# A recurrent layer whose input products are read from PSUM on VectorE, and a sparse layer whose front starts inside its last two steps

## What is computed

```python
def _lru_forward(x, ...):                       # all 4096 rows, D = 256
    u = einsum('btd,edh->ebth', x, W_in) + b_in
    in_r, in_i, o = u[0], u[1], u[2]
    nu, theta, gamma = exp(params_log)
    lam = exp(complex(-nu, theta))
    uc = complex(gamma * in_r, gamma * in_i)
    h = associative_scan(h_t = lam * h_{t-1} + uc_t)
    out = h.real @ W_mid[0] - h.imag @ W_mid[1] + (b_mid) + o
    y = gelu(out @ w1_w + w1_b) @ w2_w + w2_b + out
    return (y - mean) * rsqrt(var + eps) * ln_g + ln_b

def _gated_bottleneck(x2d, ...):                # the sparse layer's front
    xc = einsum('ngf,gf->ng', x2d.reshape(n, g, 4), conv_w) + conv_b
    xn = batchnorm over all rows of xc
    return gelu(xn) @ lin_w.T + lin_b           # scores for a top 32
```

## Time and profile before

| | us |
|---|---|
| median of 3 runs | 1512.84 (1508.34 to 1513.26) |
| the profiled execution's own time | 1514.08 |
| its span, first to last instruction | 1512.4 |
| granted TensorE clock, mean | 0.948 |

### The profile page before, as it was taken

How to read it: one execution, slowest core, us unless ns; L and a number is a source line. 1 busy time by engine, 2 the same in 40 slices (tenths; PEclk the granted TensorE clock), 3 DMA queues, 4 the chain that set the end, 5 groups by cost and what they waited for, 6 DMA issues and landing times.

```text
span 1512.4 us, 30887 instructions
## 1 busy us (share of the span) xinstructions
PE 1273.1 (84%) x10332; PEld 780.5 (52%) x10332; DVE 1175.4 (78%) x2857; ACT 1119.0 (74%) x2453; POOL 1027.2 (68%) x1137
## 2 busy tenths in 40 slices
PE   4879998877777779999999999999999999767665
PEld 2435544534445435556666566665666567334343
DVE  7989888369989978777777667776777653699997
ACT  3424333487887759998988888888888895888886
POOL 3476886328877768776777667776676772188887
PEclk9989999979899989999999999999999999799997
DMA  6100000000000000000000000000000000000000
GB/s 186 39 1 0 1 0 0 1 0 1 1 1 1 1 1 2 2 2 2 2 2 2 2 2 2 2 1 2 2 2 2 2 2 1 0 15 29 15 29 29
DMA packets 26280, 14.70 MB, mean 10 GB/s; under 512 B 14406, under 2 KB 25868, under 8 KB 26124
## 3 DMA queue, kind: packets, MB, share of 16 engines
q1 hardware_dynamic: 26124, 12.74, 3.2%
HBM read 8.47 MB, written 4.19 MB: 8 GB/s over the span
## 4 chain that ended last, share of the span: by engine, by line
PE 41%; DVE 17%; issue 15%; POOL 13%; ACT 12%; DVEq 0%; DMA 0%; SPq 0%; POOLq 0%; ACTq 0%
POOL arena L692 5%; PE banks L1715 5%; PE banks L1727 4%; PE banks L1729 4%; PE banks L1654 3%; PE banks L1677 3%; DVE arena L1294 3%; ACT arena L1006 3%; DVE arena L1196 3%; PE banks L1744 3%; DVE arena L1289 2%; PE banks L1601 2%; PE banks L1746 2%; PE banks L1745 2%; ACT arena L1014 2%
## 5 line engine op out<-in xcount | busy, mean ns | idle before, releaser
L692 POOL TENSOR_TENSOR arena<-arena 128x512 f16<-128x512 f32 x384 | 439.5, 1161 | 191.1 <-ACT arena L1014 188.7
L1006 ACT ACTIVATE arena<-banks 128x512 f32<-128x512 f32 x512 | 303.9, 599 | 85.5 <-PE banks L1729 80.7
L1380 DVE TENSOR_REDUCE arena<-banks 128x1 f32<-128x1024 f32 x256 | 309.7, 1217 | 11.0 <-PE banks L1715 7.8
L1014 ACT ACTIVATE arena<-arena 128x512 f16<-128x512 f32 x512 | 316.0, 631 | 0.1
L1744 PE MATMUL banks<-arena 128*128 128x65 f16 x2048 | 214.7, 195 | 11.9 <-POOL arena L692 11.9
L1744 PEld LDWEIGHTS banks<-arena 128*128 128x128 f16 x2048 | 190.6, 97 | 49.4 <-issue 22.3
L1745 PE MATMUL banks<-arena 128*128 128x64 f16 x2048 | 214.9, 192 | 0.0
L1746 PE MATMUL banks<-arena 128*128 128x65 f16 x2048 | 214.0, 193 | 0.0
L1397 DVE TENSOR_TENSOR arena<-arena 128x512 f16<-128x512 f32 x128 | 101.8, 796 | 141.3 <-ACT arena L1014 141.3
L1294 DVE MATCH_REPLACE8 arena<-arena 128x256 f32<-128x256 f32 x512 | 204.7, 405 | 0.7 <-issue 0.6
L1745 PEld LDWEIGHTS banks<-arena 128*128 128x128 f16 x2048 | 190.1, 99 | 27.4 <-issue 0.3
(11 more groups left out here) (201 smaller groups left out, 2757.6 us busy)
## 6 DMA issues: line engine op xcount, KB each, us to landing
x<-in_L_attn_a_x SPq DMA_DIRECT2D x8, 512.0 KB, 4.0
out<-x SPq DMA_DIRECT2D x8, 512.0 KB, 3.0
arena<-arena SPq DMA_DIRECT2D x64, 1.0 KB, 1.9
arena<-in_L_attn_a_W_in SPq DMA_DIRECT2D x1, 768.0 KB, 5.8
arena<-in_L_attn_a_W_mid SPq DMA_DIRECT2D x1, 512.0 KB, 6.7
arena<-in_L_attn_a_w_w SPq DMA_DIRECT2D x2, 256.0 KB, 6.9
arena<-in_L_attn_b_Wq SPq DMA_DIRECT2D x1, 512.0 KB
arena<-in_L_attn_b_Wo SPq DMA_DIRECT2D x1, 512.0 KB
```

Source lines behind the costliest of these rows:

```text
L692: nc.gpsimd.tensor_tensor(pr_lo[c][:, kt, :], pr[:, kt, :], pr_hi[c][:, kt, :], ALU.subtract).then_inc(a_lP, 1)
L1006: nc.scalar.activation(pr[:, kt, :], ps[6 + kt % 2][:, :], ACT.Exp, scale=SM_SCALE).then_inc(a_P, 1)
L1014: nc.scalar.activation(pr_hi[c][:, kt, :], pr[:, kt, :], ACT.Copy).then_inc(a_hi, 1)
L1380: nc.vector.tensor_reduce(mx[c][:, j:j + 1], psum[:, 2 * pair:2 * pair + 2, :].rearrange("p a b -> p (a b)"), X, ALU.max).then_inc(a_mx, 1)
```

## The change

- **PSUM read on VectorE.** ScalarE's `lru_u` is gone. VectorE's `turned_in` reads the input products out of PSUM with scalar_tensor_tensor, (ps + bias) * table, eight instructions of 128 x 512 in place of GpSimd's `products_in` and VectorE's two products. `sums` adds them up.
- **Gamma in the weights.** gamma is loaded as a row over all partitions (`gam`, one more DMA), exponentiated by ScalarE ahead of Sin, and multiplied into W_in's first two parts by GpSimd (`s_scaled`). decT is made on GpSimd, the sign of w_mid on ScalarE.
- **y.** `gain` and ScalarE's normalisation out of PSUM become `centred` on VectorE, (y - mean) * ln_g out of PSUM, and a scaling by rstd on ScalarE. `rstd2` has two instructions, not four. Banks 6 and 7 are free after `centred`.
- **Orders.** ScalarE copies outT before it normalises. VectorE's order in a step: `sums(n+1)`, half the scans, `stats2(n-1)`, `centred(n-1)`, the other scans, `turned_in(n+2)` first half, `turned_back(n+1)`, `turned_in(n+2)` second half, then statistics. The conv matrix is made in step 3, the bias rows in steps 4 and 5. The setup transposes of TensorE use two banks, not four.
- **The sparse front.** Chunks 0 to 3 are normalised, turned and partly multiplied inside steps 6 and 7 (`front_turn`, `feature_chunk`, `front_rows`, `features`); the others follow.

The diff, cut (SyncE's list, carvings, semaphores and repeated wait numbers left out):

```diff
@@ gpsimd
-            def products_in(n, c):
-                ur, ui = u[c]
-                pool.wait_ge(l_u, n * 4 + 4)
-                ...
-                nc.gpsimd.tensor_tensor(pa, ur, cosT, ALU.mult).then_inc(l_pool, 1)
-                nc.gpsimd.tensor_tensor(pb, ui, cosT, ALU.mult).then_inc(l_pool, 1)
+            def turned_back(n, part):
+                pool.wait_ge(l_dve, n * L_STEPS + 4)
+                nc.gpsimd.tensor_tensor((pa, pb)[part], g[0], (cosT, sinT)[part], ALU.mult).then_inc(l_pool, 1)
             ...
+            pool.wait_ge(s_win, 16)
+            pool.wait_ge(s_gam, 17)
+            scaled = win[:, 0:2, :, :].rearrange("p e k h -> p (e k) h")
+            nc.gpsimd.tensor_tensor(scaled, scaled, gam.unsqueeze(1).to_broadcast([P, 2 * KB2, D]),
+                                    ALU.mult).then_inc(s_scaled, 1)
             ...
             def lru_step(n, c, behind, ahead1, ahead2, ahead4):
                 if ahead1:
-                    products_in(n + 1, 1 - c)
+                    turned_back(n + 1, 0)
                 if behind:
                     rstd2(n - 1)
                 if ahead1:
-                    products_out(n + 1)
+                    turned_back(n + 1, 1)
@@ scalar
             def lru_yhat(n):
-                act.wait_ge(l_r2, n * 4 + 4)
-                ...
+                act.wait_ge(l_r2, n * 2 + 2)
                 for j in range(TPC):
-                    nc.scalar.activation(yhat[:, j, :], ps[6 + j // 2][:, D * (j % 2):D * (j % 2) + D],
-                                         ACT.Identity, bias=ynmr[:, j:j + 1],
+                    act.wait_ge(l_yc, n * TPC + j + 1)
+                    nc.scalar.activation(yhat[:, j, :], yhat[:, j, :], ACT.Copy,
                                          scale=yrs[:, j:j + 1]).then_inc(l_y, 1)
             ...
             def lru_step(n, c, behind, ahead1, ahead2, ahead4):
                 if ahead2:
                     lru_z(n + 2, c)
-                if behind:
-                    lru_yhat(n - 1)
+                if n == NCH - 2:
+                    front_rows(0)
+                if n == NCH - 1:
+                    zT_chunk(LN_FFN1 + 1, 1, 2)
+                    front_rows(2)
                 for m in range(KB2):
                     ...
-                if ahead2:
-                    lru_u(n + 2, c, (0, 1))
+                if n >= NCH - 2:
+                    zT_chunk(LN_FFN1 + 2 * (n - NCH + 2), 0, 0)
+                if behind:
+                    lru_yhat(n - 1)
                 for m in range(KB2):
                     ...
-                if ahead2:
-                    lru_u(n + 2, c, (2, 3))
+                if n >= NCH - 2:
+                    front_rows(2 * (n - NCH + 2) + 1)
             ...
-            first_rows()
+            zT_chunk(LN_FFN1 + 3, 1, 2)
+            front_rows(4)
+            zT_chunk(LN_FFN1 + 4, 0, 0)
+            front_rows(5)
             lru_yhat(NCH - 1)
+            for m in range(5, NCH):
+                zT_chunk(LN_FFN1 + m, m % 2, 2 * (m % 2))
+                if m + 1 < NCH:
+                    front_rows(m + 1)
@@ vector
+            def turned_in(n, qs):
+                wait_from(dve, l_dve, (n - 1) * L_STEPS + 2)
+                for q in qs:
+                    e, m = q // 2, q % 2
+                    dve.wait_ge(l_ups, n * 4 + q + 1)
+                    for part, table in enumerate((cosT, sinT)):
+                        nc.vector.scalar_tensor_tensor(out=turned[e][part][:, m, :], in0=ps[u_bank(n, q)][:, :],
+                                                       scalar=gbias[:, q:q + 1], in1=table[:, m, :],
+                                                       op0=ALU.add, op1=ALU.mult).then_inc(l_u, 1)
+
+            def centred(n):
+                wait_from(dve, l_x, n)
+                dve.wait_ge(l_st2, n * 8 + 8)
+                ...
+                for j in range(TPC):
+                    nc.vector.scalar_tensor_tensor(out=yhat[:, j, :],
+                                                   in0=ps[6 + j // 2][:, D * (j % 2):D * (j % 2) + D],
+                                                   scalar=ymv[:, j, 0:1], in1=lng,
+                                                   op0=ALU.subtract, op1=ALU.mult).then_inc(l_yc, 1)
             ...
             def lru_step(n, c, behind, ahead1, ahead2, ahead4):
                 if ahead1:
-                    turned_in(n + 1, 1 - c)
+                    sums(n + 1)
+                    scan(n + 1, 1 - c, 0)
                 if behind:
                     stats2(n - 1)
+                    centred(n - 1)
                 if ahead1:
-                    scans(n + 1, 1 - c)
-                if behind:
-                    gain(n - 1)
+                    scan(n + 1, 1 - c, 1)
+                if ahead2:
+                    turned_in(n + 2, (0, 1))
+                if ahead1:
+                    turned_back(n + 1, 1 - c)
+                if ahead2:
+                    turned_in(n + 2, (2, 3))
                 ...
+                if n == NCH - 1:
+                    features(0, 1)
                 if behind:
                     dve.wait_ge(l_x, n)
                     next_stats((n - 1) * TPC, (n - 1) * TPC, n - 1, TPC)
+                if n == 3:
+                    conv_matrix()
+                if n == 4:
+                    bias_row(0, 0)
+                    bias_row(32, 0)
+                if n == 5:
+                    bias_row(64, 1)
+                if n >= NCH - 2:
+                    features(0, 2 * (n - NCH + 2))
@@ tensor
             def lru_u(n, c, qs):
                 ...
-                    if not (isinstance(n, int) and n == 0 and q < 2):
-                        pe.wait_ge(l_u, n * 4 + q - 1)
+                    if n:
+                        pe.wait_ge(l_u, n * 8 + (2 * q - 2 if n > 2 or n == 2 and q > 1 else 2 * q - 6))
             ...
             def lru_step(n, c, behind, ahead1, ahead2, ahead4):
                 ...
+                if n >= NCH - 2:
+                    front_turn(n - NCH + 2)
                 ...
+                if n >= NCH - 2:
+                    feature_chunk(0, n - NCH + 2)
+                if n == NCH - 1:
+                    front_turn(2)
                 pe.wait_ge(l_o, n * 4 + 4)
-                pe.wait_ge(l_y, n * 4 + CREDIT["l_y"])
+                wait_from(pe, l_yc, n * TPC)
                 ...
+                if n == NCH - 1:
+                    feature_chunk(0, 2)
+                    front_turn(3)
                 pe.wait_ge(l_y1, n * 2 + 2)
```

More of the change, by code:

```diff
@@ L137, in hybrid_block_kernel @@
         lnb = carve([D])
+        gam = carve([D])
         sinT = carve([KB2, CH])
         decT = carve([KB2, CH])
-        u = [[carve([KB2, CH]) for _ in range(2)] for _ in range(2)]
+        front_at = room[0]
+        turned = [[carve([KB2, CH]) for _ in range(2)] for _ in range(2)]
         pa, pb = carve([KB2, CH]), carve([KB2, CH])
@@ L575, in _ @@
             rstd(0, 0)
+            pool.wait_ge(s_win, 16)
[3 more added lines that the diff above has]
+                                    ALU.mult).then_inc(s_scaled, 1)
+            pool.wait_ge(s_act0, 2)
+            nc.gpsimd.memset(decT, 0.0).then_inc(s_decay, 1)
+            pool.wait_ge(s_decay, 1)
+            for k in range(KB2):
+                nc.gpsimd.tensor_scalar(decT[:, k, :], decT[:, k, :], decay[:, k:k + 1], 0.0,
+                                        ALU.add, ALU.add).then_inc(s_decay, 1)
             rstd(1, 1)
@@ L1166, in _ @@
                 m *= 2
-            link(nc.vector.memset(decT, 0.0))
-            for k in range(KB2):
-                link(nc.vector.tensor_scalar(decT[:, k, :], decT[:, k, :], decay[:, k:k + 1], None, ALU.add))
             dve.sem_inc(s_dve0, 1)
-            def turned_in(n, c):
-                ur, ui = u[c]
-                base = n * 12
-                dve.wait_ge(l_u, n * 4 + 4)
-                if not (isinstance(n, int) and n == 0):
-                    dve.wait_ge(l_dve, base)
-                nc.vector.tensor_tensor(ta, ui, sinT, ALU.mult).then_inc(l_dve, 1)
-                nc.vector.tensor_tensor(tb, ur, sinT, ALU.mult).then_inc(l_dve, 1)
@@ new lines, in sums, with scan @@
+            def sums(n):
+                dve.wait_ge(l_u, n * 8 + 8)
+                wait_from(dve, l_dve, n * L_STEPS)
+                nc.vector.tensor_tensor(v[0], turned[0][0], turned[1][1], ALU.add).then_inc(l_dve, 1)
+                nc.vector.tensor_tensor(v[1], turned[1][0], turned[0][1], ALU.subtract).then_inc(l_dve, 1)
+            def scan(n, c, e):
+                base = n * L_STEPS
+                dve.wait_ge(l_dve, base + 1 + e)
+                for k in range(KB2):
+                    first = 0.0 if c == 0 else h[0][e][:, k, CH - 1:CH]
+                    nc.vector.tensor_tensor_scan(g[e][:, k, :], decT[:, k, :], v[e][:, k, :], first,
+                                                 ALU.mult, ALU.add).then_inc(l_dve, 1)
@@ L1345, in _ @@
```

(22 more changed lines are left out.)

216 lines of the change are left out of this document (105 added, 111 removed).

## The result

The changed kernel takes 1487.47 us (4 runs, 1485.61 to 1487.97), the kernel before 1512.44 (4 runs beside it). The ratio is 0.9838, 95% interval 0.9818 to 0.9858. The profiled execution ran 1485.61 with a span of 1483.9; 1491.6 was forecast for the span, 28.5 us went, and 20.8 had been summed up. The direction was right and the time lies inside the range; of the four terms of the sum the start and the tail came out near the forecast, the recurrent steps and steps 6 and 7 did not.

The account below looks back on a forecast made before the run. VectorE was taken to bound the steps, taking turns with GpSimd over instructions with two SBUF inputs. Gains 4.8 + 4.4 + 4.3 + 7.3 = 20.8 us took the span from 1512.4 to 1491.6; predicted 1492, range 1479 to 1506.

Parts of the forecast that it names:

- the start: Everything up to step 1: it starts at 87.6 instead of 92.4, a gain of 4.8 us, bounds 0 and 8.
- the tail: From the end of y2(7) to the first MAX8: 29 us instead of 36.3, gain 7.3, bounds 4 and 10.
- the recurrent steps: Steps 1 to 5 on VectorE: 143.3 us instead of 147.7, a gain of 4.4, bounds 14 to 0.
- steps 6 and 7: From VectorE's start of step 6 to the end of y2: 46.2 us instead of 50.5, gain 4.3.
- The unknown price of the sum: VectorE's 512-element scalar_tensor_tensor from PSUM, in no earlier row: 0.66 us back to back, bounds 0.61 and 0.70.
- Rival 3: Slower: the new VectorE instruction is dear or takes turns with GpSimd after all; 1520 to 1527 us, chance 0.08.
- the turns: VectorE and GpSimd waiting for each other's two-input instructions: 4.9 us a step on top of VectorE's 23.6.
- The 1.9 at the second scans: GpSimd's second turned_back product meets VectorE's second pair of scans: 1.9 us, with the small ones before it.
- rival 1: TensorE bounds the steps, as turns mostly fall on instructions needing none: 26.8 us a step, 1482 us, chance 0.18.
- the new wait: At the loop's end, y2 of the last chunk stands behind front_turn(3) in TensorE's order.
- Behind MAX8: The stretch after the first MAX8: only f=1's loop is unrolled, gain nothing, as it waits for ScalarE.
- a mark of being wrong: Among the listed signs of a wrong forecast: a stretch behind MAX8 that differs by more than 3 us.

Follow-up runs that it names:

- x5: Changed kernel with turned_in's eight products reading the cos table in SBUF instead of PSUM: 1497.68 us, 0.9904 of the kernel before.
- x4: Changed kernel with GpSimd's residual and add_ln_bias waiting until VectorE has written h(n+1): 1483.41 us, 0.9827 of the kernel before.
- x1: Changed kernel with the sparse layer's front moved back behind the recurrent loop: 1487.42 us, 0.9844 of the kernel before.
- second execution: The changed kernel measured again, unaltered, as the measure of scatter: 1489.05 us, 0.9867 of the kernel before; first MAX8 at 300.69.
- x8: Changed kernel with the conv matrix and three bias rows made at the end of step 0: 1489.51 us, 0.9853 of the kernel before.
- x6: Changed kernel with the turn of front chunk 3 behind y2(7) on TensorE: 1490.74 us, 0.9869 of the kernel before.
- x2: Changed kernel with ScalarE's normalisation of y back ahead of the outT copies: 1497.80 us, 0.9908 of the kernel before.
- x9: Changed kernel without gamma's exponential and GpSimd's product, so the recurrence's inputs are unscaled: 1482.03 us, 0.9816 of the kernel before.

## Why the prediction was right and where it wasn't

**Right: the instruction.** The unknown price of the sum, scalar_tensor_tensor from PSUM, was taken at 0.66 back to back and 0.75 alone, from the earlier trace rows. Measured: four in 2.70, so 0.655 from start to start, and 739 ns. The four of 256 take 1.66, where 1.6 was forecast. That it takes no turns was argued from 32 equal durations and is shown by x5. The 120 fixed cycles for a PSUM source, against 58 for SBUF, of the Trainium skill (VectorE: DVE Perf Modes, The TRN2 errata) aren't seen in the rows that answer to the earlier trace rows either (changed kernel by form, 130 to 250 us: busy, mean ns):

```profile
L1240 DVE BATCH_NORM_STATS2 arena<-banks 128x6 f32<-128x256 f32 x20 | 7.0, 411 | 0.0
L1134 DVE BATCH_NORM_STATS2 nst<-x 128x6 f32<-128x256 f32 x20 | 7.0, 409 | 0.0
```

Rival 3 falls.

**Wrong: what bounds the steps.** The prediction gave VectorE 28.6 us a step and TensorE a wait of 1.8 in each. On VectorE's edges the five took 138.3 for 143.3, and TensorE waited in one. The term that was mis-sized is the turns, 4.9 us a step. Taken from the durations beyond 2.45 for two scans and 1.21 for a product, the five steps have 15.6 us of them, 3.1 a step: second scans 6.0, L1207 3.6 (steps 2 and 3 only), L1223 and L1224 6.0. They also fall otherwise than forecast. The 1.9 at the second scans was to come in every step; it came as 0.4, nothing, nothing, 3.6 and 2.0. In steps 1 to 3 GpSimd's power (L555), itself stretched to 1.85 to 2.02 beside the scans, holds the product behind it back until they are nearly over; in steps 4 and 5 it takes 1.01 and is done when they start. Two smaller slips: 23.6 and 4.9 make 28.5, and step 3 still has ln_stats beside the conv matrix, as the earlier trace rows shows at 177.87, so it was the one step longer than forecast (28.8 for 28.4). VectorE's mean step was 27.7 instead of 28.7, less than a microsecond from TensorE's 26.7, and this excess was largely covered by VectorE's lead: only 2.6 of its 4.6 us over five steps reach TensorE, all in step 4. So rival 1, given 0.18, is what happened in all steps but one, and x4 is its pure form: 1483.4 against the 1482 that rival 1 had given.

**Wrong: steps 6 and 7.** 4.3 were forecast and 1.6 came. Counted from the o part (220.88, 247.87), step 7 took 26.5 to the end of y2, as forecast, and step 6 took 27.0 instead of 25. The two waits in step 6 are there at the forecast size, 2.42 and 0.78 for 2.4 and 1.1; the feature product behind the first of them takes 3.53, at a granted clock of 0.53, where four matmuls take 1.88 at full clock. The clock behind a wait is the term that was left out. The other 0.7 are VectorE's start of step 6, 4.6 and not 5.3 behind the o part. The tail gave 8.8 instead of 7.3. By x1 the two terms are one: work moved across the edge between them. Forecast together 11.6, measured 10.4 (11.7 by the second execution, whose last feature product took 3.60 as that of the kernel before did). A sum over a boundary that the change itself moves should be made once, for the engine that carries the work.

**Right with two errors that partly cancel: the start.** h(0) was forecast 1.4 late and came 1.25 late (60.38). Sin itself moved by 5.9 us, not 2.4, because the gamma row lands at 11.31; but VectorE had statistics to do until 10.1 in the kernel before, so its first instruction on Sin's result starts only 3.1 later (13.28 for 10.14). From there to the end of the tables it takes 22.0 for 20.0, so GpSimd's product and fills, priced at 3.3, cost some 2.0. The two together are 5.1 for a forecast of 5.7. Step 1 then starts 5.2 early for 4.8. x8 shows the cause that was named, the rows and the matrix that left the front, to be large enough: with them ahead of step 1 it starts 8.6 later. The forecast hadn't looked at TensorE's step 0, which took 35.5 before and 28.5 after. In the kernel before TensorE waits 5.93 us there for ScalarE's normalised rows (L732), which wait for GpSimd's rstd (L516) and so for statistics of VectorE, behind the bias rows in its list; w_mid(1) then takes 8.43 and not 7.05. x8 makes the rows behind those statistics, and its step 0 takes 28.2, so that their leaving ended this wait is likely and not shown:

```profile
90.80 2.08 ACT L732 ACTIVATE zrow<-x,rs 128x256 f32<-128x256 f32 x4 [11.66 <-POOL rs L516]
92.93 1.97 PE L1457 MATMUL banks<-ident,zrow 128*128 128x128 f32 x8 [5.93 <-ACT zrow L732]
```

**Wrong: the new wait.** It was named as what the change adds. x6 shows that taking it away gains nothing, and that the late turn costs 2.5 us at MAX8.

**Behind MAX8** nothing was expected and 3.4 us differ, over the 3 that the prediction had named as a mark of being wrong. The first top 8 to the first exponential of attention takes 2.0 less, attention 0.1 more; in the changed kernel's second execution the whole stretch differs from the kernel before by 1.0. Since identical code varies by 4.7 us there, this isn't put down to the change, and isn't shown to be independent of it either.

By single removals the parts weigh at MAX8, each against that execution of the changed kernel whose last feature product ran alike: PSUM source 13.4 (x5), ScalarE's order 10.8 (x2), rows out of the front 5.3 (x8), the fold -3.9 (x9), the overlap nothing (x1). They are no partition of the 26.35 between the kernel before and the second execution: either of the first two removals alone brings waits of TensorE back. Not tried: the order of VectorE's half scans, and `centred` against `gain` by itself.

## What to carry to other kernels

When three engines are nearly full, cut the profile at each engine's own recurring instruction: the one whose intervals repeat to the hundredth of a microsecond is the bound, and a step of another engine that is 1 us longer may still be covered by its lead. Here an operand in PSUM took a VectorE instruction out of the turns with GpSimd (at most 753 ns, where two SBUF operands gave up to 2829). A turn's place isn't fixed by the order of the lists alone: a small instruction of 1 or 2 us moved it from one group to the next, so look at every step and not at one. When ScalarE orders a copy that a matmul needs and a normalisation that waits for a slow engine, put the copy first; and put a table function that needs nothing ahead of one that waits for a row.

## What the runs showed of the hardware that wasn't expected

- A wait of TensorE costs more than its length when the granted clock falls behind it. After 4.76 us (x8), eight matmuls of w1 took 6.58 at a granted clock of 0.56 (3.60 at full clock); after 4.32 (before), 5.40 at 0.68; after 2.94 (x2), 5.35 at 0.69. In step 4 a wait of 2.33 was followed by 3.67 at 1.00 and, in x1 and x6, one of 2.42 by 5.37 at 0.68. The forecast had priced waits at their length everywhere but in the tail.
- The same eight feature matmuls at the same time of the same kernel took 3.60 (clock 1.00) or 5.29 (0.68): two executions can differ by 1.7 us with no difference in the program.
- GpSimd's small power of 128x4 takes 1.01 us alone and 1.85 to 2.02 beside VectorE's scans: short instructions take turns as well, and shift what stands behind them.
- Two fills of 128x512 by tensor_scalar on GpSimd take 4.00 us, as long as two products of 1024.
